# A two-layer graph network on one core: three blocks of four middle groups a layer are fetched row by row from SyncE, and their products are taken out of the sequence

## The chip, the cores and the metric

The kernel runs on 1 core of one Trainium2 chip. The metric is device time in microseconds (us); of several runs the median counts. Engines are written as in the profile: PE is TensorE (PEld its weight loads), DVE VectorE, ACT ScalarE, POOL GpSimd, SP SyncE. A "q" behind the name (DVEq) is the engine's sequencer, which does registers, branches, waits and DMA issues.

## The reference

Two SAGE convolutions, a linear layer, a residual and a layer norm over 12,500 nodes of 256 features and 200,000 edges. The edges are sorted by `dst`; `dst` is 12500 times the square of a uniform number, so nodes with small numbers have many edges. `src` is uniform.

```python
def sage(x, W_l, b_l, W_r):
    agg = segment_sum(x[src], dst, 12500)
    deg = segment_sum(ones, dst, 12500)
    return (agg / max(deg, 1)) @ W_l + b_l + x @ W_r
h = relu(sage(x, W1_l, b1, W1_r))
h = relu(sage(h, W2_l, b2, W2_r))
return layernorm(x + h @ W3 + b3)
```

## The kernel before

All arithmetic is float32. The nodes are cut into 100 windows of 125 (`WN`), the sorted edges into 1563 blocks of 128; four blocks are a group (`GB`). A layer (`layer(l, ...)`, once with rows of `x`, once with rows of `z_dram`, which is the first layer times the second's left weights) sums the rows x[src] into `acc` in two ways.

The first 348 blocks (`HB`) hold the edges into the five windows of most edges. For them the kernel counts how often each source row feeds each node (`chunk`, `count_blocks`, `keep_counts`: in layer one alone, DVE makes one-hot marks and PE multiplies them) and SP stores the counts to DRAM in parts (`store_part`). A dense product then reads all 12,500 rows in 20 steps (`STEPS`) for each of the five windows: SP's `load_step` fetches five blocks of 128 rows and the counts of the step, PE's `dense_step` (L614) multiplies them, DVE's `add_hot` (L1127) adds.

The other 304 groups (`NGG`) are gathered. POOL issues for each block one indirect DMA of 128 rows into one of four slots of `ring` (L445), and waits before a slot's first block on `s_gr` and once more before its last, until PE has consumed the group that lay there. DVE marks which edge belongs to which node of the window (`mark_group`, L1020, 128x500), PE multiplies marks and rows, four blocks into one bank (`product`, L537), and DVE adds the bank to `acc` twice under two masks (`add_masked`, L975). Groups come alternately from the front and from the back (`group_at`), so the middle groups are last. A window whose edges are all in is finished (`finish_one` after every second group): mean, the two weight products, and so on, on DVE, PE and ACT.

The order is written out in loops. The body `four` takes four groups; with `builds` it has the counting, with `dense` two dense steps, with `general` the fallback, which loads all rows once more for windows beyond five (`fallback`; with these edges its loads and a few short instructions are all that is done). Layer one: 4 groups, 48 groups that count (stage 0), then four stages of 48 groups (`STAGE`), each 8 groups that count without dense steps and 40 with; 8 groups with one fallback each; 40 groups with dense steps; 12 groups with one fallback each. Layer two: 40 groups with two fallbacks in four; five stages of 8 groups without and 40 with dense steps; 24 groups more. SP issues its loads in the order of the program, each behind a wait for the buffer half that it overwrites (`place`, on `s_xused`).

```python
                        if g >= R and b == 0:
                            pool.wait_ge(s_gr[l], g - R + 1)
                        if g >= R and b == GB - 1:
                            pool.wait_ge(s_gr[l], g - R + 2)
```

Of the kernel before, what the change touches and what calls it, by code (L numbers as in the profile page):

```python
# [22 lines left out]
N, E, D = 12500, 200000, 256  # L23
P = 128
# [45 lines left out]
TAIL_GROUPS = NGG - 4 - STAGE * (HW + 1) - STEPS + 8  # L70
# [39 lines left out]
def constants():  # L110
# [23 lines left out]
    d[:, D_POS:D_POS + NG] = np.where(g < G0 + (NGG + 1) // 2, 2 * (g - G0) + 1, 2 * (NG - g))  # L134
    d[0:NW, D_POS:D_POS + G0] = np.where(order < HW, 0, 1000)[:, None]
# [23 lines left out]
def build(nc, x, src, dst, W1l, b1, W1r, W2l, b2, W2r, W3, b3, c_f, c_s, c_win, c_node, x_turned, out):  # L159
# [5 lines left out]
    with ExitStack() as ctx:  # L165
# [10 lines left out]
        ring = sb("ring", [P, R, GB, RW])  # L176
        scol = sb("scol", [P, NC], I32)
# [23 lines left out]
        tables = sb("tables", [65, NGG * 4], I32)  # L201
        tab = tables[0:1, :]
        tabh = tables[32:33, 0:TW + 2 * NW + 1]
        win = tables[64:65, 0:NW + 1]
        eps = sb("eps", [P, 1])
# [84 lines left out]
        s_kept = sem("s_kept")  # L290

# [19 lines left out]
        def _(sp):  # L311
# [36 lines left out]
            sp.dma_start(row2, g_dram[3:5].rearrange("(o a) t g -> o a (t g)", o=1)).then_inc(s_gd, 16)  # L348

# [45 lines left out]
            sp.wait_ge(s_set, 1)  # L395
            for f in range(PARTS):
# [18 lines left out]
            fallback(x, 8, STEPS)  # L415
            for q in range(2):
                sp.wait_ge(s_zd[q], 16 * (NW // 2))
            fallback(z_dram, 0, STEPS)
            for w in range(HW):
                for t in range(STEPS):  # L420
                    load_step(z_dram, w, t)

        @block.gpsimd
        def _(pool):
            pool.memset(ed_i[:, 0, NT - 1, :], 0).then_inc(s_pad, 1)
            pool.memset(ed_i[:, 1, NT - 1, :], int(BIG)).then_inc(s_pad, 1)
            pool.memset(ring[:, :, :, D:RW], 1.0).then_inc(s_ring1, 1)
            ready = 0
            for l, rows_dram in enumerate((x, z_dram)):
# [3 lines left out]
                for g in range(NGG):  # L433
# [17 lines left out]
        def _(pe):  # L451
# [40 lines left out]
            pe.wait_ge(s_ring1, 1)  # L492
# [13 lines left out]
            for r in (fin_x, lin):  # L506
                pe.reg_mov(r, 0)
# [133 lines left out]

            def product2(j):
# [72 lines left out]
            def layer(l, dense, last):  # L715
# [8 lines left out]
                pe.reg_mov(at_row, 1)  # L724

# [17 lines left out]
                def four(builds=False, dense=False, general=()):  # L743
                    for i in range(4):
                        one_group(i, builds and i % 2 == 1)
                        if dense and i % 2 == 0:
                            dense_step(l, i // 2)
# [4 lines left out]
                        if i in general:  # L752
                            fallback(l, general.index(i) % 2)

                if l == 0:
# [7 lines left out]
                    with pe.Fori(1, HW):  # L763
                        chunk_row()
                        chunk(CJ)
                        with pe.Fori(0, STAGE // 4 - STEPS // 2):
                            four(builds=True)
                        with pe.Fori(0, STEPS // 2):
                            four(builds=True, dense=True)
                    with pe.Fori(0, 2):  # L770
                        four(general=(0, 1, 2, 3))
                    with pe.Fori(0, STEPS // 2):
                        four(dense=True)
                else:
                    with pe.Fori(0, STEPS // 2):
                        four(general=(1, 3))
                    with pe.Fori(0, HW):
# [15 lines left out]
        def _(v):  # L793
# [128 lines left out]
            for r in (hadd, xdone, fdone, fb, kept, extra):  # L922
                v.reg_mov(r, 0)
            ohf = oh.rearrange("p q b n -> p (q b n)")
# [120 lines left out]
            def group(l, i, nb, builds=False):  # L1045
# [16 lines left out]
                if i == 3:  # L1062
                    v.reg_add(gb, gb, -8)
                    turn_banks()

# [133 lines left out]
            def layer(l, dense):  # L1199
# [11 lines left out]
                v.reg_mov(at_base, 0)  # L1211
                v.load([at_tile], win[0:1, 0:1])
# [13 lines left out]
                def four(builds=False, w=None, general=()):  # L1226
                    for i in range(4):
                        group(l, i, GB, builds and i % 2 == 1)
                        if builds and i % 2:
# [4 lines left out]
                        if i in general:  # L1234
                            fallback(l)
# [5 lines left out]
                if l == 0:  # L1241
# [7 lines left out]
                    with v.Fori(0, HW - 1) as w:  # L1249
# [4 lines left out]
                        hot_chunk()  # L1254
                        with v.Fori(0, STAGE // 4 - STEPS // 2):
                            four(builds=True)
# [5 lines left out]
                    with v.Fori(0, 2):  # L1262
                        four(general=(0, 1, 2, 3))
# [3 lines left out]
                else:  # L1267
# [3 lines left out]
                    with v.Fori(0, HW) as w:  # L1271
                        with v.Fori(0, STAGE // 4 - STEPS // 2):
                            four()
                        with v.Fori(0, STEPS // 2):
                            four(w=w)
                with v.Fori(0, STEPS // 4 + (1 if l else -2)):
# [180 lines left out]
```

## Time and profile before

| | |
|---|---|
| time, median of 3 runs | 3909.38 us (3901.4 to 3915.59) |
| time of the profiled execution | 3921.47 us |
| its span | 3919.7 us |
| granted TensorE clock, mean | 0.843 of full speed |
| busy: PE, PEld, DVE, ACT, POOL | 2717.9, 2165.2, 1504.1, 477.6, 2310.3 us |
| DMA | 651.35 MB, 166 GB/s over the span |

The span is from the first instruction to the last. Layer one's gathers run from 7.2 to 2060.4 us, layer two's from 2091.8 to 3890.9 us. Busy time of POOL is the time in which it makes the descriptors of its indirect DMAs; PE's is modelled from issue times, so it is not PE at its peak. A busy share says nothing of order: what ends a wait is read from the waits and from the chain that ended last.

### The profile page before, as it was taken

How to read it: one execution, taken by the hardware profiler on the slowest of the kernel's cores; microseconds unless marked ns; L12 is line 12 of the kernel's file. 1: busy time of each engine (PE TensorE's matmuls, PEld its weight loads, DVE VectorE, ACT ScalarE, POOL GpSimd, SP SyncE). 2: the span in 40 equal slices, each digit the busy share in tenths (PEclk: the TensorE clock that was granted, in tenths of full speed). 3: DMA queues.
4: the chain of work that ended last, by engine and by line, in shares of the span. 5: the costliest groups of instructions: out<-in, count | busy, mean ns of one | idle time of the engine just before them, and what ended most of it. 6: DMA issues, size and time to landing. Idle time of an engine off the chain costs nothing.

```text
span 3919.7 us, 55770 instructions
## 1 busy us (share of the span) xinstructions
PE 2717.9 (69%) x11463; PEld 2165.2 (55%) x11464; DVE 1504.1 (38%) x3553; ACT 477.6 (12%) x1511; POOL 2310.3 (59%) x2439
## 2 busy tenths in 40 slices
PE   4655577776777767767765556777777777767766
PEld 2333355565656656646654445665656656656654
DVE  5554444454454444433322233322333323233332
ACT  2000000000000000000010111111111111111112
POOL 4445455555555656656664666666666666666664
PEclk7777789888889888988887788888888889888887
DMA  4233355656656646666664555655655655656643
GB/s 112 82 94 107 116 162 175 191 154 191 202 156 196 208 141 208 201 203 191 196 198 139 156 163 151 196 179 157 197 168 173 190 166 182 189 155 191 192 124 95
DMA packets 497280, 651.35 MB, mean 166 GB/s; under 512 B 185323, under 2 KB 415630, under 8 KB 493964
## 3 DMA queue, kind: packets, MB, share of 16 engines
q0 software_dynamic: 116736, 318.92, 27.1%
q1 hardware_dynamic: 298224, 254.51, 21.4%
q10 hardware_dynamic: 82204, 76.83, 6.6%
q14 instruction: 98, 0.80, 0.1%
q8 instruction: 18, 0.29, 0.0%
HBM read 579.62 MB, written 70.41 MB: 166 GB/s over the span
## 4 chain that ended last, share of the span: by engine, by line
DVEq 28%; issue 25%; PE 15%; another core or an unknown queue 14%; DVE 12%; POOL 3%; ACT 2%; DMA 1%; ACTq 0%; SPq 0%; PEld 0%; PEldq 0%
PE ps L537 8%; DVE acc L975 4%; DVEq L995 4%; DVEq L975 3%; PE ps L614 3%; POOL ring L445 3%; DVE oh L1020 3%; DVEq L1166 2%; DVEq L1047 2%; DVE oh L1073 2%; DVEq L986 2%; DVEq L1020 1%; DVEq L1038 1%; DVEq L1017 1%
## 5 line engine op out<-in xcount | busy, mean ns | idle before, releaser
L537 PE MATMUL ps<-ring,oh 128*125 128x257 f32 (+1 forms) x4864 | 1412.5, 442 | 657.1 <-DVE oh L1020 324.7
L445 POOL DMA_INDIRECT ring<-in_x,scol x1216 | 1158.5, 953 | 901.7 <-PE ps L537 407.6
L537 PEld LDWEIGHTS ps<-ring,oh 128*125 128x125 f32 x4864 | 1031.7, 219 | 953.6 <-issue 777.6
L445 POOL DMA_INDIRECT ring<-z_rows,scol x1216 | 1151.2, 947 | 679.3 <-issue 340.0
L975 DVE SCALAR_TENSOR_TENSOR acc<-ps,cf,acc x1224 | 544.2, 480 | 794.1 <-issue 553.6
L1020 DVE TENSOR_TENSOR oh<-dcol,ps 128x500 f32 x608 | 410.5, 675 | 610.1 <-issue 554.9
L614 PE MATMUL ps<-scratch 128*125 128x257 f32 (+1 forms) x2000 | 534.0, 410 | 86.1 <-issue 81.1
L614 PEld LDWEIGHTS ps<-scratch 128*125 128x125 f32 x2000 | 485.5, 298 | 129.5 <-issue 92.2
L588 PE MATMUL psB<-oh 128*128 (+1 forms) x546 | 189.3, 445 | 279.2 <-DVE oh L1073 197.1
L588 PEld LDWEIGHTS psB<-oh 128*128 (+1 forms) x546 | 49.3, 99 | 398.3 <-issue 376.1
L1376 ACT ACTIVATE work<-psT,b2c 128x125 f32<-128x125 f32 x200 | 62.0, 362 | 1442.7 <-remote 1162.0
L663 PEld LDWEIGHTS psY<-work,w 128*128 128x128 f32 x1600 | 222.7, 214 | 23.1 <-issue 13.9
L663 PE MATMUL psY<-work,w 128*128 128x125 f32 (+1 forms) x1600 | 220.6, 295 | 13.6 <-issue 13.6
L1335 ACT COPY work<-psY 125x256 f32<-125x256 f32 x100 | 37.2, 372 | 1522.4 <-PE psY L647 679.2
L1073 DVE TENSOR_SCALAR oh<-iota,cf,key 128x500 int16 (+1 forms) x546 | 202.3, 411 | 13.2 <-issue 12.5
L1127 DVE TENSOR_TENSOR acc<-ps,acc 125x256 f32 (+2 forms) x100 | 42.6, 426 | 328.5 <-remote 261.1
L647 PE MATMUL psY<-w,hT 128*125 128x256 f32 x400 | 134.6, 469 | 19.6 <-issue 17.5
L692 PE MATMUL psY<-w,work 128*125 128x256 f32 x400 | 115.6, 415 | 36.0 <-ACT work L1376 29.7
L707 PE MATMUL psT<-hT,w 128*128 x800 | 129.3, 282 | 15.2 <-issue 15.2
L1070 DVE TENSOR_TENSOR oh<-iota,key 128x256 int16 (+1 forms) x273 | 114.6, 420 | 51.7 <-issue 32.7
L707 PEld LDWEIGHTS psT<-hT,w 128*128 128x128 f32 x800 | 118.9, 198 | 19.0 <-issue 12.5
L1111 DVE COPY scratch<-psB 128x500 f32 x125 | 84.9, 679 | 109.7 <-issue 94.2
(140 smaller groups left out, 1107.4 us busy)
## 6 DMA issues: line engine op xcount, KB each, us to landing
scratch<-counts SPq DMA_DIRECT2D x200, 312.5 KB
scratch<-in_x SPq DMA_DIRECT2D x114, 512.0 KB
scratch<-z_rows SPq DMA_DIRECT2D x114, 512.0 KB
counts<-scratch SPq DMA_DIRECT2D x25, 1250.0 KB
ring<-in_x,scol POOLq DMA_INDIRECT x1216
ring<-z_rows,scol POOLq DMA_INDIRECT x1216
scratch<-in_x SPq DMA_DIRECT2D x114, 128.0 KB
scratch<-z_rows SPq DMA_DIRECT2D x114, 128.0 KB
```

The lines of the kernel that those rows point to most:

```text
L445: pool.indirect_dma_start(ring[:, slot, b, 0:D], None, rows_dram, bass.IndirectOffsetOnAxis(scol[:, n - C0:n - C0 + 1], 0)).then_inc(rows[ ...
L537: mm = pe.matmul(psA[0:WN, bass.ds(bank, W)], oh[:, slot, b, :], ring[:, slot, b, 0:W], start=(b == 0), stop=(b == nb - 1))
L588: mm = pe.matmul(psB[:, 0:n], oh1[:, bass.ds(at, P)], oh1[:, bass.ds(at + P, n)], start=first and b == 0, stop=True, skip_group_check=True)
L614: mm = pe.matmul(psD[0:WN, 0:W], lin_a[:, q, :, :, k].rearrange("p f n -> p (f n)"), lin_x[:, q, k, 0:W], start=(q == 0 and k == 0), stop= ...
L647: mm = pe.matmul(psZ[0:WN, 0:D], hT[:, k * WN:(k + 1) * WN], w2[:, k, 0:D], start=(k == 0), stop=(k == 1))
L663: mm = pe.matmul(psH[:, m * WN:(m + 1) * WN], w1[:, a, k, m * P:(m + 1) * P], of, start=(a == 0 and k == 0), stop=(a == 1 and k == 1))
L692: pe.matmul(at, tT[:, k, :], w3[:, k, :], start=(k == 0), stop=False)
L707: pe.matmul(psT[:, m * WN:(m + 1) * WN], w2[:, k, D + m * P:D + (m + 1) * P], hT[:, bass.ds(q + k * WN, WN)], start=(k == 0), stop=False)
L975: ins = v.scalar_tensor_tensor(out=to, in0=psA[0:WN, bass.ds(bank, W)], scalar=mask[0:WN, bass.ds(k, 1)], in1=to, op0=ALU.mult, op1=ALU.add)
L995: v.load(row, tab[0:1, bass.ds(v.snap(at, min_val=0, max_val=(NGG - 2) * 4), 8)])
L1020: v.tensor_tensor(to, cols, at, ALU.is_equal).then_inc(s_oh[l], 1)
L1073: ins = v.tensor_scalar(s[:, b, P:P + n], iota[:, table:table + n], base, key[:, 1, bass.ds(at + b, 1)], ALU.add, ALU.is_equal)
```

## The change

Four groups in the middle of the gathered edges (`G1` to `G1 + 3`, `LONE` is 4) are taken out of the alternating sequence in both layers, which has 300 groups instead of 304. Each of the four gets a product of its own.

- Their rows go to a new tile `lone`. Blocks 0 to 2 are fetched by SP: `lone_rows` loads 16 source numbers into registers at a time, from a row of `tables` (four small DMAs fill these at the start), and issues one DMA of one row (1 KB) for each, 384 a group, 3072 in all. Block 3 is fetched by POOL with one indirect DMA, put between two groups (`late`).
- SP issues them between its other work. Layer one: group 0 in three parts ahead of `store_part` 0, 2 and 4 of the first window; groups 1 to 3 one each in the passes over windows 0 to 2, 64 rows ahead of step 2, 16 behind each step, 32 behind the last. Layer two: group 0 with 16 rows behind each fallback load 2 to 15 and behind steps 2 to 11 of window 0; groups 1 to 3 in the passes over windows 1 to 3. Before a group's first row SP waits for the product of the group before it (`s_lone_mm`).
- PE's `lone_product` and DVE's `lone_mark` stand behind the second group of the first `four` of a stage, DVE's `lone_sum` at the same place of the next `four`. The product goes to `psD`, the bank of the dense product. The two `four` without dense steps carry the tests for them (`lone=True`). In layer one these are stages 1 to 4; in layer two `lone_due` is set where w is over 0, stages 1 to 4 of 0 to 4.
- The groups that are gone are taken from the last stretch of each layer: 8 instead of 12 groups in layer one, 20 instead of 24 in layer two. In layer one the 8 groups ahead of the last dense pass have 12 fallbacks instead of 8, at (0, 1, 1, 2, 3, 3) of `four`.
- `lone` and `lone_oh` take 6.1 KB a partition; the scratch for POOL's descriptors is set to 8192 (`dynamic_dma_scratch_size`).

```diff
+LONE = HW - 1
+G1 = G0 + (NGG - LONE) // 2
+BY_ROW = GB - 1
+LONE_POS = 244
-TAIL_GROUPS = NGG - 4 - STAGE * (HW + 1) - STEPS + 8
+TAIL_GROUPS = NGG - LONE - 4 - STAGE * (HW + 1) - 8
+    d[:, D_POS + G1:D_POS + G1 + LONE] = LONE_POS
+        lone = sb("lone", [P, GB, RW])
+        lone_oh = sb("lone_oh", [P, GB, WN])
...
+            for k in range(LONE):
+                e = (G1 + k) * GB * P
+                sp.dma_start(edge_rows[k], src[e:e + GB * P].rearrange("(o e) -> o e", o=1)).then_inc(s_lone_idx, 16)
...
+            regs = [sp.alloc_register(f"sp_edge{k}") for k in range(16)]
+            def lone_rows(rows_dram, l, k, j0, j1):
+                if j0 == 0 and l * LONE + k:
+                    sp.wait_ge(s_lone_mm, l * LONE + k)
+                for j in range(j0, j1, len(regs)):
+                    n = min(len(regs), j1 - j)
+                    sp.load(regs[0:n], edge_rows[k][:, j:j + n])
+                    for e in range(j, j + n):
+                        at = sp.snap(regs[e - j], min_val=0, max_val=N - 1)
+                        sp.dma_start(lone[e % P:e % P + 1, e // P, 0:D], rows_dram[bass.ds(at, 1), :]).then_inc(
+                            s_lone_row[e // P], 16)
...
             for f in range(PARTS):
+                if f in (0, 2, 4):
+                    lone_rows(x, 0, 0, *{0: (0, 160), 2: (160, 320), 4: (320, BY_ROW * P)}[f])
                 store_part(0, f)
...
-                    fallback(x, 2, 8)
+                    fallback(x, 2, 12)
...
+                if w + 1 < LONE:
+                    lone_rows(x, 0, w + 1, 0, 64)
                 for t in range(2, STEPS):
                     load_step(x, w, t)
...
+                    if w + 1 < LONE:
+                        lone_rows(x, 0, w + 1, 32 + 16 * t, 48 + 16 * t)
+                if w + 1 < LONE:
+                    lone_rows(x, 0, w + 1, 32 + 16 * STEPS, BY_ROW * P)
...
+            for t in range(STEPS):
+                fallback(z_dram, t, t + 1)
+                if 2 <= t < 16:
+                    lone_rows(z_dram, 1, 0, 16 * (t - 2), 16 * (t - 1))
             for w in range(HW):
                 for t in range(STEPS):
                     load_step(z_dram, w, t)
+                    if w == 0 and 2 <= t < 12:
+                        lone_rows(z_dram, 1, 0, 192 + 16 * t, 208 + 16 * t)
+                    if 0 < w < LONE and t:
+                        lone_rows(z_dram, 1, w, *((0, 64) if t == 1 else (32 + 16 * t, 48 + 16 * t)))
+                if 0 < w < LONE:
+                    lone_rows(z_dram, 1, w, 32 + 16 * STEPS, BY_ROW * P)
...
-                for g in range(NGG):
+                late = [8] + [(4 if l == 0 else 40) + STAGE * k + STAGE // 2 for k in range(1, LONE)]
+                for g in range(NGG - LONE):
+                    if g in late:
+                        k = late.index(g)
+                        n = (G1 + k + 1) * GB - 1
+                        if l * LONE + k:
+                            pool.wait_ge(s_lone_mm, l * LONE + k)
...
+                        pool.indirect_dma_start(
+                            lone[:, GB - 1, 0:D], None, rows_dram,
+                            bass.IndirectOffsetOnAxis(scol[:, n - C0:n - C0 + 1], 0)).then_inc(s_lone_pool, 16)
...
+            def lone_product(l):
...
+                dense_free()
+                for b in range(BY_ROW):
+                    pe.wait_ge(s_lone_row[b], landed)
+                pe.wait_ge(s_lone_pool, turned)
...
+                pe.wait_ge(s_lone_oh, n)
+                for b in range(GB):
+                    mm = pe.matmul(psD[0:WN, 0:W], lone_oh[:, b, :], lone[:, b, 0:W],
+                                   start=(b == 0), stop=(b == GB - 1))
+                mm.then_inc(s_lone_mm, 1)
+                next_lone()
...
+            def lone_mark(l):
...
+                v.tensor_tensor(lone_oh[:], cols, at, ALU.is_equal).then_inc(s_lone_oh, 1)
...
+            def lone_sum(l):
...
+                v.wait_ge(s_lone_mm, n)
+                v.wait_ge(s_ad[l], cv)
+                lone_add(l, *place).then_inc(s_lone_ad, 1)
+                v.wait_ge(s_lone_ad, n)
+                v.sem_inc(s_dbank, 1)
+                next_lone()
...
-                        four(general=(0, 1, 2, 3))
+                        four(general=(0, 1, 1, 2, 3, 3))
...
+                        pe.reg_alu(lone_due, w, 0, ALU.is_gt)
                         with pe.Fori(0, STAGE // 4 - STEPS // 2):
-                            four()
+                            four(lone=True)
...
-                with pe.Fori(0, STEPS // 4 + (1 if l else -2)):
+                with pe.Fori(0, STEPS // 4 if l else 2):
...
-    nc = bacc.Bacc("TRN2", target_bir_lowering=False, num_devices=1)
+    nc = bacc.Bacc("TRN2", target_bir_lowering=False, num_devices=1, dynamic_dma_scratch_size=8192)
```

## Rows read from the trace of the kernel before

**Rows 1.** The page: span; busy time; the chain by engine.
```profile
span 3919.7 us, 55770 instructions
PE 2717.9 (69%) x11463; PEld 2165.2 (55%) x11464; DVE 1504.1 (38%) x3553; ACT 477.6 (12%) x1511; POOL 2310.3 (59%) x2439
...
DVEq 28%; issue 25%; PE 15%; another core or an unknown queue 14%; DVE 12%; POOL 3%; ACT 2%; DMA 1%; ACTq 0%; SPq 0%; PEld 0%; PEldq 0%
```

**Rows 2.** Windows, layer one: counting without dense, with dense, last stretch.
```profile
core 0: us, PE busy (x) PEld busy (x) DVE busy (x) ACT busy (x) POOL busy (x), PEclk, DMA share, GB/s
...
1419.00:1470.00 51.00, 36.30 (x180) 28.13 (x181) 26.01 (x64) 6.22 (x20) 31.41 (x34) 0.97 0.52 147
...
1470.00:1693.00 223.00, 168.78 (x757) 135.83 (x755) 101.92 (x242) 17.20 (x55) 136.10 (x144) 0.89 0.66 204
...
1988.00:2062.00 74.00, 47.90 (x210) 38.69 (x209) 22.38 (x68) 7.76 (x25) 45.27 (x48) 0.82 0.67 206
```

**Rows 3.** Windows, layer two: with dense, without dense, last stretch.
```profile
2684.00:2921.00 237.00, 173.43 (x739) 145.37 (x739) 70.06 (x154) 39.61 (x133) 150.03 (x159) 0.86 0.63 190
2921.00:2968.00 47.00, 33.64 (x128) 27.46 (x127) 14.00 (x30) 7.89 (x27) 30.35 (x33) 0.72 0.39 112
...
3750.00:3892.00 142.00, 95.04 (x387) 74.88 (x386) 43.10 (x93) 24.77 (x83) 90.91 (x96) 0.83 0.39 111
```

**Rows 4.** Timeline of POOL in a stretch without dense steps.
```profile
2664.91 0.94 POOL L445 DMA_INDIRECT ring<-z_rows,scol  x1 [0.30 <-issue]
2666.15 0.94 POOL L445 DMA_INDIRECT ring<-z_rows,scol  x1 [0.30 <-issue]
2670.74 0.94 POOL L445 DMA_INDIRECT ring<-z_rows,scol  x1 [3.65 <-remote]
```

**Rows 5.** The page's costliest groups: product, adds, marks, dense step.
```profile
L537 PE MATMUL ps<-ring,oh 128*125 128x257 f32 (+1 forms) x4864 | 1412.5, 442 | 657.1 <-DVE oh L1020 324.7
...
L975 DVE SCALAR_TENSOR_TENSOR acc<-ps,cf,acc x1224 | 544.2, 480 | 794.1 <-issue 553.6
L1020 DVE TENSOR_TENSOR oh<-dcol,ps 128x500 f32 x608 | 410.5, 675 | 610.1 <-issue 554.9
L614 PE MATMUL ps<-scratch 128*125 128x257 f32 (+1 forms) x2000 | 534.0, 410 | 86.1 <-issue 81.1
```

**Rows 6.** Timeline of SP: two loads of one partition; one dense step.
```profile
2.28 0.23 SPq L321 DMA_DIRECT2D acc<-in_src  x1
...
20.58 0.25 SPq L342 DMA_DIRECT2D tables<-c  x1
...
2510.66 0.36 SPq L374 DMA_DIRECT2D scratch<-counts  x1
2511.07 0.53 SPq L351 DMA_DIRECT2D scratch<-z_rows  x1
2511.63 0.51 SPq L355 DMA_DIRECT2D scratch<-z_rows  x1
```

**Rows 7.** Sequencer steps of DVE by line: ns min/median/max.
```profile
L1020 DVEq FUSED_REGOPS  x608: 2/99/774, 45.7 to 3891.7; - x152
...
L995 DVEq TENSOR_LOAD <-tables x306: 3/814/2936, 43.0 to 3892.0; - x153
```

**Rows 8.** The chain in order of time, 2654 to 2672 us.
```profile
2661.74 0.70 DVEq L1054
2662.45 0.71 DVEq L995
```

**Rows 9.** The chain in order of time where the last dense pass begins.
```profile
1764.91 0.38 SPq L351
...
1766.52 6.35 DMA scratch<-counts
```

**Rows 10.** SP's waits; the DMA queue of instructions (packets, MB, share).
```profile
SPq L374 <- remote: 1146.8, 88, 59.5
...
q14 instruction: 98, 0.80, 0.1%
```

More of the change, by code:

```diff
@@ L204, in build @@
         win = tables[64:65, 0:NW + 1]
+        edge_rows = [tables[96 + k // 2:97 + k // 2, k % 2 * GB * P:(k % 2 + 1) * GB * P] for k in range(LONE)]
         eps = sb("eps", [P, 1])
@@ L427, in _ @@
             pool.memset(ring[:, :, :, D:RW], 1.0).then_inc(s_ring1, 1)
+            pool.memset(lone[:, :, D:RW], 1.0).then_inc(s_ring1, 1)
             ready = 0
@@ L506, in _ @@
             for r in (fin_x, lin):
+                pe.reg_mov(r, 0)
+            lone_row = [pe.alloc_register(f"pe_lone_row{k}") for k in range(4)]
+            lone_at, lone_n, lone_rows, lone_turn, lone_due = (
+                pe.alloc_register(f"pe_{v}") for v in ("lone_at", "lone_n", "lone_rows", "lone_turn", "lone_due"))
+            for r in (lone_n, lone_rows, lone_turn):
                 pe.reg_mov(r, 0)
@@ L741, in one_group, with four @@
                         pe.reg_add(turn, turn, 16 * GB)
-                def four(builds=False, dense=False, general=()):
+                def four(builds=False, dense=False, general=(), lone=False):
                     for i in range(4):
                         one_group(i, builds and i % 2 == 1)
+                        if lone and i == 1:
+                            with pe.If(0 < pe.snap(lone_due)):
+                                lone_product(l)
                         if dense and i % 2 == 0:
@@ L751, in four @@
                             finish_one(row_of(i)[3])
-                        if i in general:
-                            fallback(l, general.index(i) % 2)
+                        for n, at in enumerate(general):
+                            if at == i:
+                                fallback(l, n % 2)
                 if l == 0:
@@ L923, in _ @@
                 v.reg_mov(r, 0)
+            lone_row = [v.alloc_register(f"v_lone_row{k}") for k in range(3)]
+            lone_at, lone_n = (v.alloc_register(f"v_{q}") for q in ("lone_at", "lone_n"))
+            lone_due = v.alloc_register("v_lone_due")
+            v.reg_mov(lone_n, 0)
             ohf = oh.rearrange("p q b n -> p (q b n)")
@@ L1064, in group, with lone_place, lone_add @@
                     turn_banks()
+            def lone_place(w, off):
+                return v.snap(w, min_val=0, max_val=NW) * RW, v.snap(off, min_val=0, max_val=WN)
+            def lone_add(l, at, k):
+                W = RW if l == 0 else D
+                for shift, mask in ((0, upper), (RW, lower)):
+                    to = acc[0:WN, bass.ds(at + shift, W)]
+                    ins = v.scalar_tensor_tensor(out=to, in0=psD[0:WN, 0:W], scalar=mask[0:WN, bass.ds(k, 1)],
+                                                 in1=to, op0=ALU.mult, op1=ALU.add)
+                return ins
@@ L1224, in finish_one, with four @@
                         v.reg_add(fin, fin, 1)
-                def four(builds=False, w=None, general=()):
+                def four(builds=False, w=None, general=(), lone=False):
                     for i in range(4):
                         group(l, i, GB, builds and i % 2 == 1)
+                        if lone and i == 1:
+                            with v.If(1 < v.snap(lone_due)):
+                                lone_sum(l)
+                            with v.If(0 < v.snap(lone_due)):
+                                lone_mark(l)
                         if builds and i % 2:
@@ L1233, in four @@
                             finish_one(row_of(i)[3])
-                        if i in general:
-                            fallback(l)
+                        for at in general:
+                            if at == i:
+                                fallback(l)
                     if w is not None:
```

78 lines of the change are left out of this document (68 added, 10 removed).

## The prediction

> **What bounds the kernel now.** I read the page first. POOL is busy 59% of the span, PE 69%, DVE 38%, and the chain by engine gives POOL 3% but DVE's sequencer 28%, "issue" 25%, PE 15% and unnamed queues 14% [rows 1]. No engine is full; the reader is to see a loop of several engines. So I asked next, by windows, how fast the loop turns in each kind of stretch, with the count of POOL's fetches as the clock, since every group costs four. Layer one, counting: 51 us for 34 fetches without dense steps and 223 for 144 with them, 1.50 and 1.55 us each; in its last stretch 74/48 = 1.54 [rows 2]. Layer two: 237/159 = 1.49 with dense steps, 47/33 = 1.42 without, 142/96 = 1.48 in the last stretch [rows 3]. POOL's timeline says why layer two hardly changes: a fetch is 0.94 us and a gap of 0.30, so POOL alone would take 1.25 each, and every dozen or so it waits some microseconds for PE to free a slot, 3.65 in the row shown [rows 4]. The loop is thus POOL's own pace for 85% (1.25 of 1.48) and a wait for the PE and DVE side for the rest.
>
> The chain in order of time shows what that side does in such a wait: DVE's sequencer takes 0.70 us for steps (a register operation, a load of a table row) that have a median of 0.10 for a register operation elsewhere [rows 7, 8]. The profile doesn't name the cause. It matters, because the change adds such steps.
>
> What a taken-out group is worth is therefore its whole turn, not POOL's busy time: 16 fetches, four groups, are 16 x 1.48 = 23.7 us in layer two's last stretch and 16 x 1.54 = 24.7 us in layer one's, where the change takes them out. That is the credit, **48.4 us**.
>
> **What the change adds.**
>
> *POOL's fourth blocks.* Eight fetches. In layer one they stand where POOL waits for others anyway (1.55 against 1.25), so 0; in layer two 4 x 1.25 = 5.0 us, bounds 0 and 8 x 1.48 = 11.8. I take **5.0**.
>
> *The products.* PE does four blocks, 1412.5 us over 608 groups = 2.3 us; DVE one mark of 0.68 and two adds of 0.48, 1.6 us [rows 5]. The sequencers add, by my count in the code, some 25 steps on DVE and 20 on PE, at 0.10 about 2.5 us on DVE, and a load of a table row each, 0.8 [rows 7]. Wholly exposed, one after the other on DVE, that is 1.6 + 2.5 + 0.8 = 4.9; PE's 2.3 + 2.0 + 0.8 = 5.1 runs beside it; call it 5.1. But they stand in the two `four` of a stage that have no dense steps, and there the trace has a measure of what extra work costs. A `four` with dense steps has two of them more on PE, 534.0/200 x 2 = 5.3 us [rows 5], and lasts 16 x (1.49 - 1.42) = 1.1 us longer in layer two and 16 x (1.55 - 1.50) = 0.8 in layer one [rows 2, 3]. A product has half of that PE work, but more on DVE, and DVE is busier in layer one (101.9/223 = 46%) than in layer two (70.1/237 = 30%). I take 2 us a product in layer two and 3 in layer one, 8 + 12 = **20 us**; bounds 0 and 8 x 5.1 = 41. The tests in the `four` without a product are in this. What is queued behind the product is PE's next group, and behind that POOL's slot; POOL is 12 to 16 fetches ahead, which is the cover. Without it the price is the 5.1.
>
> *SP's rows.* 3072 DMAs of one row. No row shows one with an address from a register. Two loads of a single partition were issued in 0.23 and 0.25 us [rows 6]; with a register step of 0.10 and a gap of 0.04 a row is 0.4 us. Sixteen are 6.4, and a load of 16 numbers about 0.9 (8 words took 0.81 [rows 7]), 7.3 us. A `four` has two such bursts and two dense steps of 0.36 + 0.53 + 0.51 = 1.4 us [rows 6]: 14.6 + 2.8 = 17.4 us of SP in 23.7. It fits, and a load is issued at most one burst later than now, with a buffer half that is freed 12 us before its neighbour. SP sits idle now: one of its waits alone sums to 1146.8 us [rows 10]. The 64 rows ahead of step 2, 29 us, lie in the 8 groups without dense steps (47 us). What is queued behind a late row is every later dense load, and PE's `dense_step` for it. I take **0**. Lower bound 0; the upper is the second rival. The same bytes leave POOL's queue, so DMA traffic is as before; a dense pass alone moves the DMA share from 0.39 to 0.63 and the fetch only from 1.42 to 1.49 [rows 3], so the rows' share can't be much.
>
> A rule speaks against this part. The Trainium skill ("Runtime: NRT & Kernel Launch", Instruction fetch mechanics) says that a register load costs about 200 ns for each register, even in bulk. By it 16 would be 3.2 us, a `four` would need 22.0 us of SP's time, and the sum would stay, with almost no room. The trace has 8 words in 0.81 and disagrees, though its loads read SBUF.
>
> *The last dense pass of layer one.* Today PE's first step of it already waits for SP: the rows are issued at 1764.91, behind a fallback, and the counts take 6.35 us on the chain [rows 9]. With three fallbacks in each two groups the load of step 0 is freed one group later, at (3, 3) of `four` instead of (2). A group is 5.9 to 6.2 us. Bounds 0 and 6.2, and up to 6 more if six loads in a `four` land late; I take **4**.
>
> *The smaller scratch, the start.* POOL never has more than 16 fetches under way. If half the scratch still holds them it costs 0; if not, POOL's 0.30 gap would grow. Each 0.01 us on 2408 fetches is 24 us, and that is the one edit whose upper bound no row gives. I take 0. Four small loads and a memset at the start lie under the preparation, 0.
>
> **The sum.** -48.4 + 5.0 + 20 + 0 + 4 = -19.4 us, against the profiled execution's 3921.5: 3902.1. The shown runs' median is 3909.4, 0.31% under that execution, so the prediction is 3909.4 x 3902.1/3921.5 = **3890 us**.
>
> **Rivals.**
>
> *The products are paid in full (no change).* At 5.1 each: -48.4 + 5.0 + 41 + 4 = +1.6, 3911 us. For it: DVE's sequencer and "issue" are over half of the chain [rows 1], so DVE work may be worth its whole length. Against: the dense steps' extra work costs a fifth of its length.
>
> *SP falls behind (slower).* Place: SP between two dense loads. In a `four` it has 23.7 us, less 2.8 for the loads and 1.8 for the register loads, for 32 rows: it decides at 19.1/32 = 0.60 us a row. At 0.75 a `four` with rows takes 28.6 instead of 23.7; there are 67 of them (27 in layer one, 40 in layer two), +330 us, 4200. For it: steps of 0.70 on another sequencer [rows 8]. Against: 0.23 and 0.25 as issued.
>
> *Slow steps around the products (slower).* Place: DVE in `lone_mark` and `lone_sum`, new bodies of 25 steps. If half run at 0.70, a product costs 1.6 + 0.8 + 1.3 + 8.4 = 12 us, eight 97: -48.4 + 5 + 97 + 4 = +58, 3967 us. It decides where a product costs (48.4 - 9)/8 = 4.9 us. For it: such runs occur in most turns of the loop. Against: they end in a wait that is there already, and the turn of 1.48 holds with few or many. The Trainium skill (same page and section) has a rule that would do it: a taken branch whose target lies outside the two pages at hand stops the engine for a fetch. The tests that skip the new bodies are such branches. The trace's instruction queue moved only 98 packets in the whole span [rows 10], so the loops' branches before don't behave so; longer bodies may.
>
> *Everything hides (faster still).* -48.4 + 5.0 = -43.4, 3866 us.
>
> **Chances and range.** Measurement tells about 0.3% (11.7 us) from no change. My forecast, products half hidden or better, 0.60, its own range 3864 to 3900; products in full 0.19; SP behind 0.08; slow steps or the scratch 0.13. Up to 3922 the range takes in the second case and the milder ends of the third and fourth. Faster 0.61, same 0.19, slower 0.20.
>
> **What would show it.** POOL: 2408 fetches, still 0.94 and 0.30; if the gap grows it is the scratch. SP: 3072 DMAs named `lone`, starts 0.4 apart. The windows of the `four` with a product: 1.42 to 1.6 us a fetch; much more, and the products are paid. PE's waits for `scratch` (L614 before): under 15 us in sum; hundreds mean that SP is late. The last stretches: 8 and 20 groups at the same pace. The prediction is wrong if rows cost over 0.60, if the fetch pace in dense stretches moves by 0.02 us (over 2408 fetches that is 48 us), or if a product costs 5.

## The result and the profile after

The changed kernel takes 4415.37 us (4397.7 to 4430.22, 4 runs), the kernel before 3905.39 (3894.56 to 3915.59) beside it: a ratio of 1.1301, 95% interval 1.1265 to 1.1337. Forecast was 3890. The second rival, SP falls behind, came true, and beyond its 4200.

The page of the kernel after: span, busy time, the queue of instructions, the chain by engine and by line, then three of the costliest groups.
```profile
span 4428.4 us, 65321 instructions
...
PE 2778.9 (63%) x11463; PEld 2200.7 (50%) x11464; DVE 1502.7 (34%) x3553; ACT 477.6 (11%) x1511; POOL 2290.4 (52%) x2416
...
q14 instruction: 191, 1.56, 0.1%
...
SPq 20%; issue 18%; PE 7%; another core or an unknown queue 6%; DVEq 5%; DVE 2%; DMA 1%; ACT 1%; PEld 0%; ACTq 0%; PEldq 0%
SPq L415 12%; SPq L414 4%; PE ps L601 3%; SPq L412 2%; PE ps L678 2%; DMA scratch<-z_rows 1%; SPq L369 1%; SPq L365 1%; DVEq L1106 1%; DVE acc L1086 1%; PE psY L762 1%; DVE oh L1131 1%; SPq L388 1%; DVEq L1086 1%
...
L504 POOL DMA_INDIRECT ring<-z_rows,scol x1200 | 1136.7, 947 | 1028.3 <-PE ps L601 461.3
L601 PE MATMUL ps<-ring,oh 128*125 128x257 f32 (+1 forms) x4800 | 1359.9, 435 | 574.7 <-DVE oh L1131 275.7
L678 PE MATMUL ps<-scratch 128*125 128x257 f32 (+1 forms) x2000 | 639.0, 476 | 635.4 <-DMA scratch<-z_rows 369.8
```
SP's sequencer, 0% of the chain before [rows 1], leads it now, with the lines of the rows: L412 loads 16 numbers, L414 is the register operation, L415 the transfer with its move. POOL does less than before at the same 947 ns a fetch, and idles over 1000 us in each layer. The dense step (L678) is the victim: PE stood idle before it for 86.1 us in all [rows 5] and now for 635.4, and 549.7 of these ended with the landing of a dense load's rows (369.8 in layer two, 179.9 in layer one). That is the sign the prediction named.

SP's timeline in layer two, one stage with rows (start, length, instruction; x16 is a burst of 16 rows):
```profile
3353.92 0.40 SPq L388 DMA_DIRECT2D scratch<-counts  x1
3354.37 0.52 SPq L365 DMA_DIRECT2D scratch<-z_rows  x1
3354.93 0.50 SPq L369 DMA_DIRECT2D scratch<-z_rows  x1
3356.82 6.97 SPq L415 DMA_DIRECT2D lone<-z_rows  x16
3363.85 0.40 SPq L388 DMA_DIRECT2D scratch<-counts  x1
...
3366.74 17.32 SPq L415 DMA_DIRECT2D lone<-z_rows  x16
3384.11 0.39 SPq L388 DMA_DIRECT2D scratch<-counts  x1
...
3387.76 7.57 SPq L415 DMA_DIRECT2D lone<-z_rows  x16
...
3398.28 17.45 SPq L415 DMA_DIRECT2D lone<-z_rows  x16
3415.78 0.40 SPq L388 DMA_DIRECT2D scratch<-counts  x1
```
No row carries a bracket with a wait: SP goes from burst to load to burst and is never ahead. In a whole stage of 372 us (2918 to 3290) these are all of its waits:
```profile
SPq L412 <- PE ps L736: 1.8, 1, 1.8
SPq L388 <- PE ps L678: 0.2, 1, 0.2
```
Two dense steps, one turn of four groups, take 3384.11 - 3353.92 = 30.2 us and then 31.7, where before four groups took 23.7. And the same 16 rows are sent in 7 us or in 17.

The lines of a row (ns min/median/max), and the chain in order of time inside the burst of 17.32 us:
```profile
L415 SPq DMA_DIRECT2D lone<-z_rows x1536: 2/228/1421, 2274.8 to 4018.5; - x192
...
L414 SPq FUSED_REGOPS  x3072: 2/44/1436, 42.5 to 4018.4; - x192
...
L412 SPq TENSOR_LOAD <-tables x192: 4/1167/3972, 41.3 to 4010.5; - x192
```
```profile
3374.38 0.71 SPq L415
3375.14 0.70 issue
3375.84 0.71 SPq L415
3376.59 0.72 SPq L414
3377.30 0.71 issue
```
The medians are what I had put together, 0.42 us a row in all. In the long bursts the time goes in pieces of 0.70. The view lists the longest pieces alone; between them stand steps of 0.00 to 0.05. Measured from one step's start to the next, in the 67 bursts of over 15 us, about a third of the steps (1122 of 3015) last over 0.6 us and hold 84% of the time. It is the piece that DVE's sequencer showed before [rows 8], now on SP. It wasn't DVE's own before either; PE's sequencer had it too, in a register operation with a median of 47 ns:
```profile
L537 PEldq FUSED_REGOPS  x608: 3/47/1386, 46.6 to 3894.4; - x152
```
Of all register operations before, 616 of DVE's and 168 of PE's last 0.66 to 0.76 us. POOL's timeline at that place (the bracket is its idle time before, and what ended it):
```profile
3366.06 0.94 POOL L504 DMA_INDIRECT ring<-z_rows,scol  x1 [25.25 <-PE ps L601]
3367.30 0.95 POOL L504 DMA_INDIRECT ring<-z_rows,scol  x1 [0.30 <-issue]
...
3388.08 0.95 POOL L504 DMA_INDIRECT ring<-z_rows,scol  x1 [0.30 <-issue]
3397.57 0.94 POOL L504 DMA_INDIRECT ring<-z_rows,scol  x1 [8.55 <-PE ps L601]
```
POOL fetches from 3366 to 3389 with pauses of 1.4 and 2.5 us at most, and SP's steps stretch from about 3367 on; the burst that ends in POOL's pause is short again. Over the whole trace, steps of over 0.6 us hold 0.20 of SP's time in the rows while POOL pauses, 0.46 in the first 2 us of a run of fetches without a break of 0.6 us, and 0.98 once the run has lasted 6 us. That goes together, but it is not a cause shown, and it can't be the whole one: in the trace of the same program that takes 3169 us (below), POOL fetches without a break nearly all the time and such steps hold 0.01.

**One thing is needed to read the experiments.** They ran in several batches, each on one chip, and the batches fall in two sorts by the time of the unchanged kernel before: 3856 to 3905 us (the first comparison and two of the later ones, here "slow-step batches"), and 3175 to 3182 (the other five, "quick batches"). Each ratio is against before in the same batch. Whether the chip itself makes the sort isn't known: number 6 is on record for a slow-step batch (3856 us) and, eleven minutes later, for a quick one (3175). The recorded expectations speak of chips.

### The profile page after: what moved, and what is told of

Same layout as the page of the kernel before. It is cut to its first block, busy times and chain, and to the rows that moved or that the text cites. A ratio compares the mean times of both kernels' runs of the same rounds, so it can differ in the third digit from the quotient of the medians.

```text
span 4428.4 us, 65321 instructions
## 1 busy us (share of the span) xinstructions
PE 2778.9 (63%) x11463; PEld 2200.7 (50%) x11464; DVE 1502.7 (34%) x3553; ACT 477.6 (11%) x1511; POOL 2290.4 (52%) x2416
## 4 chain that ended last, share of the span: by engine, by line
SPq 20%; issue 18%; PE 7%; another core or an unknown queue 6%; DVEq 5%; DVE 2%; DMA 1%; ACT 1%; PEld 0%; ACTq 0%; PEldq 0%
SPq L415 12%; SPq L414 4%; PE ps L601 3%; SPq L412 2%; PE ps L678 2%; DMA scratch<-z_rows 1%; SPq L369 1%; SPq L365 1%; DVEq L1106 1%; DVE acc L1086 1%; PE psY L762 1%; DVE oh L1131 1%; SPq L388 1%; DVEq L1086 1%
## 5 line engine op out<-in xcount | busy, mean ns | idle before, releaser
L601 PE MATMUL ps<-ring,oh 128*125 128x257 f32 (+1 forms) x4800 | 1359.9, 435 | 574.7 <-DVE oh L1131 275.7
L504 POOL DMA_INDIRECT ring<-in_x,scol x1200 | 1145.5, 955 | 1073.8 <-PE ps L601 601.5
L504 POOL DMA_INDIRECT ring<-z_rows,scol x1200 | 1136.7, 947 | 1028.3 <-PE ps L601 461.3
L601 PEld LDWEIGHTS ps<-ring,oh 128*125 128x125 f32 x4800 | 1013.5, 217 | 840.6 <-issue 663.3
L678 PE MATMUL ps<-scratch 128*125 128x257 f32 (+1 forms) x2000 | 639.0, 476 | 635.4 <-DMA scratch<-z_rows 369.8
L678 PEld LDWEIGHTS ps<-scratch 128*125 128x125 f32 x2000 | 523.7, 306 | 743.4 <-DMA scratch<-z_rows 391.4
L1086 DVE SCALAR_TENSOR_TENSOR acc<-ps,cf,acc x1208 | 534.4, 480 | 1031.7 <-PE ps L601 481.1
L652 PE MATMUL psB<-oh 128*128 (+1 forms) x546 | 180.2, 432 | 205.4 <-DVE oh L1237 143.7
```

The lines of the kernel that those rows point to most:

```text
L504: pool.indirect_dma_start(ring[:, slot, b, 0:D], None, rows_dram, bass.IndirectOffsetOnAxis(scol[:, n - C0:n - C0 + 1], 0)).then_inc(rows[ ...
L601: mm = pe.matmul(psA[0:WN, bass.ds(bank, W)], oh[:, slot, b, :], ring[:, slot, b, 0:W], start=(b == 0), stop=(b == nb - 1))
L652: mm = pe.matmul(psB[:, 0:n], oh1[:, bass.ds(at, P)], oh1[:, bass.ds(at + P, n)], start=first and b == 0, stop=True, skip_group_check=True)
L678: mm = pe.matmul(psD[0:WN, 0:W], lin_a[:, q, :, :, k].rearrange("p f n -> p (f n)"), lin_x[:, q, k, 0:W], start=(q == 0 and k == 0), stop= ...
L1086: ins = v.scalar_tensor_tensor(out=to, in0=psA[0:WN, bass.ds(bank, W)], scalar=mask[0:WN, bass.ds(k, 1)], in1=to, op0=ALU.mult, op1=ALU.add)
```

## The experiments

**Theory one:** SP's sequencer is out of time in each turn with rows, so that dense loads come late. **Theory two:** it is the traffic of 3072 transfers of one row. **Theory three:** the products, the packed fallback passes or the smaller scratch.

### First batch: parts of the change, in a quick batch

The scratch alone, in the kernel before:
```diff
-nc = bacc.Bacc("TRN2", target_bir_lowering=False, num_devices=1)
+nc = bacc.Bacc("TRN2", target_bir_lowering=False, num_devices=1, dynamic_dma_scratch_size=8192)
```


> The kernel before with nothing but the smaller scratch for POOL's descriptors. If the scratch carries part of the loss, this run is slower than 3905 us by that part and POOL's gap of 0.30 us between two fetches grows. If it carries none, as every other theory has it, 3905 us within 0.3%.

3174.82 us, ratio 0.9998 (0.9988 to 1.0008): the scratch costs nothing.

No single rows; each 16 are one transfer of 16 consecutive rows, so the sums of the eight groups are of other rows (the count of landed transfers that PE waits for is adapted, here and with half of the rows):
```diff
-sp.load(regs[0:n], edge_rows[k][:, j:j + n])
-for e in range(j, j + n):
-    ... one row from the address in a register
+sp.dma_start(lone[e % P:e % P + n, e // P, 0:D], rows_dram[e:e + n, :])
```


> The changed kernel, but each 16 single-row DMAs and the register load ahead of them are one DMA of 16 consecutive rows, so the sums are those of other rows; bytes, products, waits and the order of the work stay. Theory one (SP's sequencer has too little time between two dense loads, because each row costs it three steps, a register operation, a move and the DMA): the loss is gone, 3890 us, what was forecast when SP keeps up. Theory three (the products, their tests and the packed fallbacks cost the time): it stays near 4400. Theory two (many single-row transfers hold up the other transfers) also says 3890.

Half of the rows singly, the other 8 of each 16 as one transfer of consecutive rows:

> As the run before, but of each 16 rows the first 8 are fetched singly by number and the other 8 with one DMA of consecutive rows (other rows' sums). Theory one is a limit: SP needs 2 x (1.2 + 8 x 0.89) + 2.8 = 19.4 us in a turn of four groups that lasts 23.7 to 25, so nearly all of the loss is gone, 3890 to 3950 us. Theory two is in proportion to the rows: half of the 510 us stays, about 4150.

All rows singly, but from fixed rows, without the load, the operation and the move:
```diff
-sp.load(regs[0:n], edge_rows[k][:, j:j + n])
 for e in range(j, j + n):
-    at = sp.snap(regs[e - j], min_val=0, max_val=N - 1)
-    sp.dma_start(lone[...], rows_dram[bass.ds(at, 1), :])
+    sp.dma_start(lone[...], rows_dram[e:e + 1, :])
```


> The changed kernel with all 3072 single-row DMAs, but each from a row that is fixed when the kernel is built, so without the load of 16 numbers, the register operation and the move (other rows' sums). Theory one: a third of the steps, about 8 us for 16 rows instead of 14, 19 us in a turn of 23.7: 3890 to 3960 us. Theory two: as many transfers of the same size, so 4415.

They gave 0.9998 (0.9987 to 1.0008), 0.9987 (0.9978 to 0.9997) and 0.9992 (0.9982 to 1.0002), 3172 to 3177 us. Nothing could be told from them, since before took 3175.76 us in this batch; whether the loss exists there had to be asked first.

### The change itself in quick batches

> The changed kernel itself once more. On the chip of the first comparison the kernel before takes 3905 us and DVE's and SP's sequencers take 0.70 us for many steps; on the chip of the four runs above it takes 3176 us, POOL never waits and hardly a step of 0.70 is seen. Theory one says that the loss comes from such steps: where the kernel before takes about 3905 us this run takes 4415; where it takes about 3176, SP needs 2 x 7.9 + 2.8 = 18.6 us in a turn of 20.1, so it just keeps up and the time is 3170 to 3190. Theory two (3072 single-row transfers hold up the others) says 13% slower on either chip, 3590 us on the fast one.

3168.66 us against 3176.38, ratio 0.9978 (0.9968 to 0.9988); in a later one 3169.0 against 3175.36, 0.9983 (0.9973 to 0.9992), expected thus:

> The changed kernel beside the two below. Theory one (SyncE's sequencer) and theory two (the traffic of single rows) both expect the loss again on a chip where before takes 3850 to 3910: ratio 1.13, 4360 to 4415 us; 0.998 where before takes 3176.

The same program loses 13% in one sort of batch and gains 0.2% in the other. In the second of these two batches, the steps of a row, the chain by engine and the dense step are:
```profile
L414 SPq FUSED_REGOPS  x3072: 44/44/59, 41.4 to 2808.5; - x192
...
L415 SPq DMA_DIRECT2D lone<-z_rows x1536: 224/228/334, 1648.2 to 2808.6; - x192
...
POOL 37%; issue 20%; PE 19%; DVEq 8%; DMA 7%; DVE 5%; SPq 4%; ACT 0%; PEld 0%; PEldq 0%; ACTq 0%; POOLq 0%
...
L678 PE MATMUL ps<-scratch 128*125 128x257 f32 (+1 forms) x2000 | 487.7, 392 | 11.0 <-DMA scratch<-counts 8.6
```
and its SP timeline:
```profile
2290.97 6.61 SPq L415 DMA_DIRECT2D lone<-z_rows  x16
2298.52 0.39 SPq L388 DMA_DIRECT2D scratch<-counts  x1
```
Bursts are 6.6 us, and added up over the trace's 192 bursts (first row's issue to last row's end) they average 6.7 there against 12.6 in the first comparison. A turn of SP is two bursts, and for each 1.5 us of dense loads and 1.5 of register load and gaps: 2 x (6.7 + 3.0) = 19.4 us. POOL alone needs 16 x 1.25 = 20.0 for a turn. It fits by 0.6 us, and PE waits 11.0 us for the dense step's data in the whole span.

The kernel before in that batch, expected and then read (one run, 3179.97 us):

> The kernel before itself, for a profile on the same chip as the three below. Its median on the last chip was 3855.8 us, on the first 3905.4: I expect layer two's turn of four groups at about 23.4 us where the last chip is met, 20.1 us where it is the chip of 3176 us.

```profile
L1020 DVEq FUSED_REGOPS  x608: 93/99/123, 43.7 to 3143.6; - x152
...
2480.00:2720.00 240.00, 197.06 (x880) 168.81 (x881) 84.71 (x187) 47.55 (x160) 181.49 (x193) 0.91 0.70 210
```
DVE's operation of the marks, 2/99/774 before [rows 7], never exceeds 123 ns, and no register operation of DVE or PE exceeds 229: there are no pieces of 0.70. Four groups take 20.0 us, and the clock is granted at 0.91 there against 0.86 in [rows 3].

### More and fewer steps for each row, in a slow-step batch

```diff
 for e in range(j, j + n):
+    for _ in range(6):        # 2 in the second kernel
+        sp.sem_inc(s_idle, 1)
     at = sp.snap(regs[e - j], min_val=0, max_val=N - 1)
```


> The changed kernel, with six increments of an unused semaphore ahead of each single row on SyncE: nothing is fetched or computed otherwise, only the row costs SyncE's sequencer more. I take an increment at 0.07 to 0.1 us, so that a row of 0.42 us (its time in the repeat of the changed kernel, where the median steps are those of the first profile) becomes 0.84 to 1.02 us and a burst of 16 with its register load 14.6 to 17.5 us. Theory one (SyncE's sequencer is out of time in each turn of four groups): on the chip of the repeat, where a turn without the rows takes 20.1 us, a turn needs 2 x 14.6 + 2.8 = 32 to 38 us in the 67 turns that hold rows, so 800 to 1200 us more than the repeat's 3169: 3970 to 4370 us, the loss of the first comparison made anew where the chip does not make it by itself. On the chip of the first comparison it is worse than 4415. Theory two (the traffic of 3072 transfers of one row): the traffic is unchanged, and even more spread out, so the time stays at 3169 us there. Theory three (products, packing, scratch): unchanged too, 3169.

> The same with two increments ahead of each row: 0.56 to 0.62 us a row, a burst of 10.1 to 11.1 us, a turn of 2 x 10.1 + 2.8 = 23 to 25 us. By theory one, on the chip of the repeat (20.1 us a turn) 67 turns lose 3 to 5 us each: 200 to 330 us more, 3370 to 3500; the point at which the rows begin to cost is (20.1 - 2.8) / 2 = 8.65 us a burst, 0.47 us a row. Theories two and three: no change, 3169.

> Of each 16 rows 8 go singly and 8 as one transfer of consecutive rows (these are other rows than the graph's, so the sums of those groups are others). Sent beside the slowed rows because it is the opposite dose: on the chip of the first comparison a burst of 9 transfers at 0.89 us plus the load is 8.6 us, a turn of SyncE 20 us, under the 23.7 us of a turn, so 3880 to 3920 us by theory one; by theory two half of the loss, about 4150. On the chip of the repeat 3169 by all theories.

Before took 3855.8 us here; half of the rows ran once more in this batch. Six increments: 5661.77 us, ratio 1.4659 (1.4618 to 1.4701). Two: 4805.69, 1.2455 (1.2424 to 1.2485). Half of the rows: 3944.01, 1.0234 (1.0206 to 1.0263). The traffic of the first two is that of the change. A stage of 48 groups in layer two, by windows, for two increments, six and half of the rows (length, busy PE, PEld, DVE, ACT, POOL, clock, DMA share, GB/s):
```profile
3157.00:3586.00 429.00, 217.40 (x880) 177.97 (x880) 86.19 (x187) 44.58 (x150) 183.47 (x194) 0.74 0.40 119
```
```profile
3717.00:4234.00 517.00, 225.83 (x862) 182.63 (x862) 87.02 (x188) 44.57 (x150) 182.96 (x194) 0.70 0.33 98
```
```profile
2666.00:2963.00 297.00, 208.32 (x862) 171.56 (x862) 88.69 (x188) 44.59 (x150) 182.81 (x194) 0.86 0.58 171
```
and the changed kernel in the first comparison, a stage with rows and the last one, without:
```profile
2918.00:3290.00 372.00, 211.69 (x862) 174.97 (x862) 87.17 (x187) 44.53 (x150) 182.93 (x194) 0.77 0.46 137
...
4040.00:4323.00 283.00, 206.74 (x855) 171.89 (x854) 86.44 (x185) 44.53 (x150) 181.65 (x193) 0.86 0.56 170
```
A twelfth of a stage is a turn. SP's need is again 2 x (burst + 3.0), with the mean of the 24 bursts in this stage, and the last column has all of SP's waits in it:

| kernel | burst | SP needs | turn measured | SP waits, in the stage |
|---|---|---|---|---|
| half of the rows | 9.1 us | 24.2 us | 24.8 us (297) | 3.0 us |
| the change | 12.6 | 31.2 | 31.0 (372) | 2.0 |
| two increments | 15.0 | 36.1 | 35.8 (429) | 2.2 |
| six increments | 18.2 | 42.4 | 43.1 (517) | 2.2 |
| the change, stage without rows | - | 3.0 | 23.6 (283) | - |

From some 24 us on, the turn is SP's need, to 3%, and SP hardly waits. With half of the rows SP is just at that point, which its 8 single rows don't explain at their median price: they are stretched too. The sizes expected of the slowed rows were for a quick batch, which they didn't meet; for this sort only "worse than 4415" was on record. An increment is 0.06 us (rows of 0.55 and 0.78 us at the median), and the mean lies above it by the stretched steps (0.99 and 1.27 us a row; 0.83 in the change, with a median of 0.43).

### The traffic alone

The kernel with fixed addresses was run again until it met a slow-step batch: it keeps all 3072 single transfers.

> All 3072 transfers of one row stay, but from fixed rows, without the register load, the register operation and the move of each (the rows are not the graph's, so the sums of these groups are others). Theory one: a row is one step of 0.3 us, of 0.7 us where the step is slow; a burst of 16 is 5 us at best and 11 us at worst, a turn of SyncE 13 to 25 us against 23.4: on a chip of 3855 to 3905 no loss or a small one, 3870 to 3950 us. Theory two (traffic of single rows): all of it is still there, 4360 to 4415.

> Each 16 rows as one transfer of 16 consecutive rows (other rows than the graph's, so the sums of these groups are others), with no register load: the packets of 1 KB stay, the single transfers go, and GpSimd is still relieved of its 24 fetches. Theory one and two: no loss; what is left is what products and packing cost less 24 fetches: products alone gave 1.0117 of before on the last chip, 49 us; less 24 fetches at 1.48 us that is 1.003 of before, 3865 us there, if a fetch taken away is paid back in full, and 1.012 if it isn't.

> All 3072 transfers of one row stay, from fixed rows, without the register load, the register operation and the move (other rows than the graph's). If the chip is one on which before takes 3850 to 3910 us: by theory one a burst is 5 us at best and 11 at worst, so 3870 to 3950 us; by theory two, for which single-row traffic makes the loss, 4360 to 4415 us. If it is one of 3176 us, 3170 by both, and nothing is told apart.

> As the run before it of this kernel: on a chip of 3850 to 3910 us theory one gives 3870 to 3950 us and theory two 4360 to 4415; on one of 3176 both give 3170.

These four met quick batches: 0.9994 (0.9984 to 1.0005), 1.0011 (1.0 to 1.0021), 0.9982 (0.997 to 0.9994), 0.9999 (0.9984 to 1.0014). Also half of the rows once more, beside the first repeat of the change: 0.9982 (0.9971 to 0.9992), 3171.25 us where 3172 was expected for such a batch. Then:

> As before: on a chip of 3850 to 3910 us theory one gives 3870 to 3950 us and theory two 4360 to 4415; on one of 3176 both give 3170.

3933.79 us against 3859.66 (two runs against three), ratio 1.02 (1.0131 to 1.0268), in theory one's range; theory two wanted 4360 or more. Its bursts average 7.5 us, so SP needs 2 x (7.5 + 1.5) = 18 us a turn, with no register load. A stage, and SP's waits in it:
```profile
2667.00:2963.00 296.00, 201.46 (x863) 169.32 (x864) 88.62 (x190) 44.53 (x150) 182.48 (x194) 0.86 0.57 171
```
```profile
SPq L388 <- remote: 43.9, 8, 14.3
SPq L388 <- PE ps L676: 12.8, 6, 4.2
```
24.7 us a turn: the loop's pace, not SP's, which waits 56.7 us of the 296. The number of single-row transfers doesn't make the loss of 13%. One thing more differs here: the rows are consecutive ones of DRAM, not scattered. No run tells that apart by itself, but with increments alone the scattered traffic stays the same and the turn grows with SP's need.

### Products and packing alone

POOL fetches all four blocks of each of the eight groups; SP sends no rows:
```diff
-pool.indirect_dma_start(lone[:, GB - 1, 0:D], ...)
+for b in range(GB):
+    pool.indirect_dma_start(lone[:, b, 0:D], ...)
```


> The changed kernel without the rows on SyncE: GpSimd fetches all four blocks of each of the six groups, where the change lets it fetch the fourth. Products, marks, packed fallback passes, scratch and every other part stay, and every sum is computed. Theory one: no loss on either chip; what is left is the cost of products and packing against before. On the chip of the repeat a fetch is 1.25 us with its gap, so taking 18 fetches back costs up to 22 us against the changed kernel: 3190 if they are paid in full, and 3176 (before) if the arrangement by itself costs nothing. On the chip of the first comparison 3890 to 3925. Theory three (products, packing or scratch make the loss) : on the chip of the first comparison about 4400, on the other one unchanged at 3169.

The text counts six groups and 18 fetches; they are eight and 24. In the slow-step batch it took 3904.93 us, ratio 1.0117 (1.009 to 1.0144), 49 us over before, so theory three falls for the loss of 13%. Two stages with a product and one without:
```profile
2932.00:3227.00 295.00, 210.97 (x890) 176.60 (x890) 87.22 (x189) 50.46 (x170) 185.80 (x197) 0.86 0.58 175
3227.00:3522.00 295.00, 207.22 (x888) 173.62 (x888) 88.75 (x193) 47.49 (x160) 185.33 (x197) 0.85 0.57 173
3522.00:3803.00 281.00, 208.39 (x858) 173.55 (x859) 87.66 (x187) 44.53 (x150) 181.90 (x193) 0.84 0.57 172
```
A stage with a product is 14 us longer, of which its four fetches are 4 x 1.48 = 5.9, which leaves 8 us for the product; the whole 49 us over eight products are 6 each.

> GpSimd fetches all four blocks of each of the eight groups (24 fetches more than in the changed kernel; the expectation of the first run of this kernel said six groups and 18 fetches, which was a miscount), no rows on SyncE. Where before takes 3176 us, GpSimd is never idle for long and a fetch with its gap is 1.25 us: if the 24 fetches and nothing else part it from the changed kernel (3169), it takes 3169 + 30 = 3199; then products and packing cost 23 us of the 30 that the fetches save. If the arrangement is hidden there it takes 3176. Where before takes 3856, 1.012 of before again.

In a quick batch, 3199.07 us, ratio 1.0068 (1.0051 to 1.0085), as the first branch of the expectation had it. A stage with a product there, and the wait that it makes for POOL:
```profile
1892.00:2139.00 247.00, 199.09 (x888) 170.07 (x888) 86.99 (x188) 47.56 (x160) 184.15 (x196) 0.90 0.69 206
...
2113.31 0.94 POOL L498 DMA_INDIRECT ring<-z_rows,scol  x1 [3.74 <-PE ps L595]
```
247 - 240 is 7 us, four fetches 5.0, a product 2.

## Why the prediction was wrong, step by step

**SP's rows, "I take 0": this is the step that failed.** The row at its fastest was right (0.42 for 0.4, a burst with its load 8.0 us for 7.3), and nothing speaks against the point at which it decides (0.60). What failed is that I costed it by two loads issued at the very start of the program, in 0.23 and 0.25 us [rows 6], and left the 0.70 us steps of the chain [rows 8] to DVE. A row is three sequencer steps, each of which can be stretched: its mean became 0.83. At that value my own formula gives 32 x 0.83 + 2.8 + 1.8 = 31.2 us a turn; measured 31.0. So the cost was mis-sized, and with it the overlap that was to hide it: the dense loads behind the bursts came late. The second rival had the place right and took 0.75 a row; its sum of +330 us is 4220 by my own terms, not the 4200 on record. With the 67 turns I had counted, and 31.0 against the 24.6 of products alone (295/12), 429 us are explained; the loss beyond products and packing is 4415 - 1.0117 x 3905 = 464. The rest presumably lies in bursts outside those turns, such as the 64 rows in one go ahead of step 2, which took 76 us here where I had put 29:
```profile
3277.98 75.89 SPq L415 DMA_DIRECT2D lone<-z_rows  x64
```
That the loss follows the steps of SP and not the number of transfers is shown by the four doses, SP's missing waits and the fixed addresses. That POOL's stream of fetches stretches the steps is only argued, and why quick batches don't show it is open. The rule of the Trainium skill on register loads ("Runtime: NRT & Kernel Launch", Instruction fetch mechanics: about 200 ns a register, so 3.2 us for 16) isn't borne out here either: 16, loaded from SBUF, took 1.17 at the median.

**The products, 2 to 3 us each.** In quick batches the size came out: products only cost 3199.07 - 3176.3 = 22.8 us, where my terms for products and the last dense pass sum to 24. But I had worked it out for the loop of 23.7 us a turn, and in a slow-step batch they cost 49: there the first rival, products paid in full, would have been the better term (41 + 4). The agreement in the other sort is luck.

**The last dense pass of layer one, 4 us.** Too little. POOL's waits in the quick batch around it, in the change and then in before:
```profile
1346.06 0.95 POOL L504 DMA_INDIRECT ring<-in_x,scol  x1 [5.97 <-PE ps L601]
...
1383.21 0.94 POOL L504 DMA_INDIRECT ring<-in_x,scol  x1 [9.78 <-PE ps L601]
```
```profile
1363.85 0.94 POOL L445 DMA_INDIRECT ring<-in_x,scol  x1 [6.38 <-PE ps L537]
```
One wait of 6.4 has become two of 6.0 and 9.8, 9 us more; the products are then some 1.7 us each.

**The credit.** 32 fetches taken out at the loop's turn, eight put back: in quick batches the change against products only is 3199.1 - 3169 = 30 us for 24 fetches, 1.25 each, POOL's own pace and all of it. With the 23 us of products and packing that makes the -7 us measured. In slow-step batches the credit didn't show: half of the rows and fixed addresses took 1.023 and 1.020 of before, against 1.0117 with 24 fetches more, which are 36 us at the loop's pace. With half of the rows SP had no time left (3.0 us of waits in 297), and PE's wait before the dense step is 169.2 us against 80.6. With fixed addresses SP had time and PE waited 72.4, and yet the 36 us are missing; the intervals of the two kernels touch, so no more than that can be said, and the reason is not settled.

**The scratch, 0; the gap of 0.30 and the 0.94 of a fetch unchanged.** Right, by the first experiment and by every trace. **Fetching of code:** q14 went from 98 packets to 191; the stretched steps occur in the chain of before too, in loops, and in a quick batch the same program, with the same 191 packets, has none, so nothing points to it.

## What to carry to other kernels

An idle engine is idle by the mean of its steps, not by their median: before giving an idle queue thousands of short instructions, divide the time of a turn by their number and ask whether the worst step seen on any sequencer would still fit. When one engine issues for two consumers in a fixed order, the price of being late is not its own work but the other consumer's, here the dense load behind each burst, turn after turn. And where a change lives on a small margin, repeat it at other times and on other chips: 0.6 us of room in a turn of 20 held in one sort of batch and was gone in the other. A list of the longest pieces of a chain leaves out the short ones: read next to it how many steps there are.

## What the hardware showed that I had not expected

- The same kernel before took 3905, 3856 and 3860 us in three comparisons and 3175 to 3182 in the other five. The longer times go with pieces of 0.70 us on the sequencers of DVE, PE and SP; the shorter with no register operation above 0.23 on DVE or PE. The number of one chip stands with both.
- In slow-step batches one row from an address in a register cost SP 0.42 us or, stretched, up to 4.3 (over 2 in 318 of 2880 rows); in the mean 0.83. A fixed address took 0.30 at the median, 7.5 us for 16.
- A load of 16 registers from one partition of SBUF took 1.17 us, a semaphore increment 0.06.
